# First attention stage: score products by query and by key in 32-row strips, with one PSUM pair for key fills and two for query fills

## The reference, cut to what matters

```python
x = x + 0.5 * ffn(layernorm(x)); x = x + attn(layernorm(x)); ...
Q, K, V = heads(x @ Wq), heads(x @ Wk), heads(x @ Wv)          # 16 heads of 8 features
scores = einsum('bhqd,bhkd->bhqk', Q, K) / sqrt(8)
scores = where(causal_mask, -1e6, scores)
attn = einsum('bhqk,bhkd->bhqd', softmax(scores), V)
return attn.reshape(b, s, 128) @ Wo + bo
```

## Time and profile before

| | |
|---|---|
| runs, us | 2098.77, 2099.65, 2094.84; median 2098.77 |
| the profiled execution's own time | 2099.55 us |
| its span, first to last instruction | 2097.6 us |
| busy over the span | PE 1996.0, PEld 1441.4, DVE 1634.0, ACT 1199.7, POOL 929.9 us |
| the chain that ended last | PE 64%, DVE 11%, issue 10%, POOL 8%, ACT 3% |
| granted TensorE clock, mean | 0.982 of full speed |
| first score product of `attn0` starts | 342.6 us |
| last key product of `attn0` starts | 715.7 us |

### The profile page before, as it was taken

The page is one execution under the profiler, slowest core; times in us unless marked ns, Lnnn a source line. Parts: engine busy times, 40 slices in busy tenths (PEclk is TensorE's granted clock), DMA queues, the critical chain, the costliest instruction groups (busy, mean ns, idle before and its releaser), DMA issues.

```text
span 2097.6 us, 44742 instructions
## 1 busy us (share of the span) xinstructions
PE 1996.0 (95%) x10752; PEld 1441.4 (69%) x10752; DVE 1634.0 (78%) x3337; ACT 1199.7 (57%) x1736; POOL 929.9 (44%) x904
## 2 busy tenths in 40 slices
PE   6999998999999889999999999998999989999998
PEld 4777776666666677777777888875333348877787
DVE  6777777777777667777668888886777788888887
ACT  6667664555555666666544544555766654544444
POOL 4565563333233356666534444442122334444444
PEclk9999999999999999999999999999999999999999
DMA  6233333333333233444301111113343401111112
GB/s 205 95 118 110 103 122 106 98 96 98 90 83 87 64 113 121 120 124 122 113 23 50 46 44 45 45 46 117 99 130 95 125 27 41 46 45 45 40 51 71
DMA packets 120701, 179.29 MB, mean 85 GB/s; under 512 B 33840, under 2 KB 38576, under 8 KB 120496
## 3 DMA queue, kind: packets, MB, share of 16 engines
q1 hardware_dynamic: 120624, 178.37, 27.8%
HBM read 147.10 MB, written 31.20 MB: 85 GB/s over the span
## 4 chain that ended last, share of the span: by engine, by line
PE 64%; DVE 11%; issue 10%; POOL 8%; ACT 3%; DVEq 1%; DMA 1%; SPq 1%; POOLq 1%; ACTq 0%
PE pair L392 14%; PE pair L394 13%; PE pair L393 13%; POOL h_lo L1356 5%; PE bank L644 4%; PE pair L733 3%; PE pair L755 3%; PE bank L622 3%; PE pair L816 2%; PE bank L392 2%; PE bank L394 1%; PE bank L393 1%; DVE rmax L1181 1%; DVE h_hi L1124 1%; POOL h_lo L1362 1%
## 5 line engine op out<-in xcount | busy, mean ns | idle before, releaser
L1362 POOL TENSOR_TENSOR h_lo<-hid,h_hi 128x512 fp32r<-128x512 f32 x256 | 335.5, 1310 | 417.0 <-ACT h_hi L913 416.9
L1356 POOL TENSOR_TENSOR h_lo<-hid,h_hi 128x512 fp32r<-128x512 f32 x256 | 331.6, 1299 | 219.7 <-ACT h_hi L879 219.4
L392 PE MATMUL pair<-xnT_hi,w_hi 128*128 (+1 forms) x1040 | 421.7, 405 | 4.8 <-DVE prod L1103 3.2
L394 PE MATMUL pair<-xnT_hi,w_lo 128*128 (+1 forms) x1040 | 408.7, 393 | 0.0
L393 PE MATMUL pair<-xnT_lo,w_hi 128*128 (+1 forms) x1040 | 408.4, 393 | 0.0
L908 ACT ACTIVATE hid<-pair,bias 128x512 f32<-128x512 f32 x256 | 176.6, 690 | 319.0 <-PE pair L394 276.0
L392 PE MATMUL pair<-h_hi,w_hi 128*128 128x512 f32 x784 | 313.4, 400 | 29.5 <-ACT yT L866 12.6
L394 PE MATMUL pair<-h_hi,w_lo 128*128 128x512 f32 x784 | 307.4, 392 | 0.0
L393 PE MATMUL pair<-h_lo,w_hi 128*128 128x512 f32 x784 | 307.0, 392 | 0.0
L1103 DVE SCALAR_TENSOR_TENSOR prod<-pair,bias,wb 128x512 f32<-128x512 f32 x256 | 191.0, 746 | 76.9 <-PE pair L394 61.4
L1124 DVE TENSOR_SCALAR h_hi<-pair,nb 128x512 fp32r<-128x512 f32 x256 | 191.1, 746 | 75.1 <-PE pair L394 72.3
(11 more groups left out here) (163 smaller groups left out, 3238.8 us busy)
## 6 DMA issues: line engine op xcount, KB each, us to landing
wb<-parts_dram SPq DMA_DIRECT2D x512, 128.0 KB, 2.8
wb<-parts_dram SPq DMA_DIRECT2D x128, 256.0 KB, 3.2
parts_dram<-attn_parts SPq DMA_DIRECT2D x96, 256.0 KB, 3.0
attn_q_st<-parts_dram SPq DMA_DIRECT2D x64, 256.0 KB, 2.7
k_one<-parts_dram SPq DMA_DIRECT2D x128, 64.0 KB, 2.4
attn_k_st<-parts_dram SPq DMA_DIRECT2D x32, 256.0 KB, 3.1
stage_w<-in_w_dram SPq DMA_DIRECT2D x32, 130.0 KB, 2.5
stage_w<-in_w_dram SPq DMA_DIRECT2D x5, 512.0 KB, 6.0
```

What stands on the lines that cost most here:

```text
L392: eng.matmul(o, w_hi_, v_hi, start=start, stop=False, **kw)
L394: return eng.matmul(o, w_lo_, v_hi, start=False, stop=stop, **kw)
L1356: eng.tensor_tensor(h_lo[:, p % NH0, :], hid[:, unit_of(p) % NHID, :] if p else hs[:, :], h_hi[:, p % NH0, :].bitcast(F32), ALU.subtract). ...
L1362: eng.tensor_tensor(h_lo[:, j % NH1, :], hid[:, j // 2 % NHID, :], h_hi[:, j % NH1, :].bitcast(F32), ALU.subtract).then_inc(lo1p_ready, 1)
```

## The change

In `attn0` alone. Each product by query or by key now takes only the 32 rows of its head's strip, for two heads of a fill; the two further heads of fill 4 still take all 128 rows, since they share a bank with the first two. Key fills all use pair 2; query fills and maxima alternate on pairs 0 and 1. In slots of kinds 0 to 3 PE now waits for both pairs and then issues the query fill's two heads and the key fill's two heads, which lie in the four different strips (key fills 2 and 3 have changed places for that, and `pv0` looks its fill up), then the rest of the query fill and the masks. In slots of kind 4 the key fill comes first, and then the query fill. The values of fill 4 come after the key fill, and the maxima move from the middle of kind 4 to the end of kind 3 (`MAX_AT`); on ACT the write-back L918 comes behind the exponential of its slot.

```diff
-K_FILLS = ((0, ((0, 0),)), (1, ((0, 0),)), (0, ((1, P), (3, 0))), (1, ((1, P), (3, 0))), (None, ((2, 0),)))
+K_FILLS = ((0, ((0, 0),)), (1, ((0, 0),)), (1, ((1, P), (3, 0))), (0, ((1, P), (3, 0))), (None, ((2, 0),)))
-MAX_AT = (4, 9, 14, 19)
+MAX_AT = (3, 8, 13, 18)
+QUERY_USES = tuple(u for n in range(NS0) for u in (("q", n),) + ((("max", n),) if n in MAX_AT else ()))
...
-    return (USES.index((what, n % NS0)) - (len(USES) if n < 0 else 0)) % NPAIR
+    return 2 if what == "k" else QUERY_USES.index((what, n % NS0)) % 2
...
+        def wait_pair(eng, ch, use):
+
+            what, n = use
+            if what == "k":
+                if n:
+                    eng.wait_ge(*filled(ch, ("k", n - 1)))
+                elif not ch.first:
+                    eng.wait_ge(*filled(ch.before(), ("k", NS0 - 1)))
+                return
+            for other in reversed(QUERY_USES[:QUERY_USES.index(use)]):
+                if ring(other) == ring(use) and in_chunk(ch, other):
+                    return eng.wait_ge(*filled(ch, other))
...
+        def strip(j):
+            return slice(PC * j, PC * (j + 1))
+
+        def query_scores(eng, quad, fill, j, b, rows_, first=True):
+
+            at0 = 256 * (j // 2) if fill == NF - 1 else 0
+            for i, (qt, at) in enumerate(Q_FILLS[fill][1]):
+                w, at = (qt + 1) * P, at + at0
+                eng.matmul(pair[b][:, j % 2, at:at + w], mem0.q_st[rows_, quad, qt * P:(qt + 1) * P],
+                           mem0.k_one[rows_, quad, j, 0:w], start=(i == 0 and first), stop=True, skip_group_check=True)
...
+            wait_pair(eng, ch, ("k", n))
+            keys, late = list(heads_in(K_FILLS, fill)), n - 1 in MAX_AT
+            if late:
+                for i, j in enumerate(keys):
+                    ins = key_scores(eng, quad, fill, j, ring(("k", n)), strip(j) if i < 2 else slice(0, P), i < 2)
+                ins.then_inc(st_ready, 1)
             if owner is not None:
-                eng.wait_ge(*last_reader(ch, ("q", n)))
-                scores_by_query(eng, owner, f, ring(("q", n)))
-            if n in MAX_AT and in_chunk(ch, ("max", n)):
-                eng.wait_ge(*last_reader(ch, ("max", n)))
-                maxima_to_rows(eng, ch if max_quad(n) < NQ else ch.after(), max_quad(n) % NQ, ring(("max", n)))
+                if f % NF == 0:
+                    eng.wait_ge(st_in[f // NF], stacks_in(owner))
+                wait_pair(eng, ch, ("q", n))
+                queries = list(heads_in(Q_FILLS, f % NF))
+                beside = [j for j in keys if j not in queries[:2]][:2]
+                for j in queries[:2]:
+                    query_scores(eng, f // NF, f % NF, j, ring(("q", n)), strip(j))
+                keys = beside + [j for j in keys if j not in beside]
+            if not late:
+                for i, j in enumerate(keys):
+                    ins = key_scores(eng, quad, fill, j, ring(("k", n)), strip(j) if i < 2 else slice(0, P), i < 2)
+                ins.then_inc(st_ready, 1)
+            if owner is not None:
+                for j in queries[2:]:
+                    query_scores(eng, f // NF, f % NF, j, ring(("q", n)), slice(0, P), False)
+                mask_queries(eng, f % NF, ring(("q", n)))
             if quad and fill == 1:
                 pv0(eng, ch, quad - 1, 2)
-            if n == NF - 1 and ch.first:
-                eng.wait_ge(x_done, ONE + ch.s * NB)
-            eng.wait_ge(*last_reader(ch, ("k", n)))
-            scores_by_key(eng, ch, n, ring(("k", n)))
             if fill == NF - 1:
                 pv0(eng, ch, quad, 0)
                 pv0(eng, ch, quad, 1)
+            if n in MAX_AT and in_chunk(ch, ("max", n)):
+                wait_pair(eng, ch, ("max", n))
+                maxima_to_rows(eng, ch if max_quad(n) < NQ else ch.after(), max_quad(n) % NQ, ring(("max", n)))
```

More of the change, by code:

```diff
@@ L124 @@
 Q_FILLS = ((0, ((3, 0),)), (1, ((3, 0),)), (0, ((2, 0), (0, 384))), (1, ((2, 0), (0, 384))), (None, ((1, 0),)))
-K_FILLS = ((0, ((0, 0),)), (1, ((0, 0),)), (0, ((1, P), (3, 0))), (1, ((1, P), (3, 0))), (None, ((2, 0),)))
+K_FILLS = ((0, ((0, 0),)), (1, ((0, 0),)), (1, ((1, P), (3, 0))), (0, ((1, P), (3, 0))), (None, ((2, 0),)))
 LOAD = 1024
-MAX_AT = (4, 9, 14, 19)
-USES = tuple(u for n in range(NS0) for u in (("q", n),) + ((("max", n),) if n in MAX_AT else ()) + (("k", n),))
-AHEAD_USES = tuple((what, n - NS0) for what, n in USES if n >= NS0 - AHEAD and what != "k" and (what, n) != ("max", MAX_AT[-2]))
+MAX_AT = (3, 8, 13, 18)
+QUERY_USES = tuple(u for n in range(NS0) for u in (("q", n),) + ((("max", n),) if n in MAX_AT else ()))
+AHEAD_USES = tuple((what, n - NS0) for what, n in QUERY_USES if n >= NS0 - AHEAD and (what, n) != ("max", MAX_AT[-2]))
 def max_quad(n):
-    return (n + 1) // NF
+    return (n + 2) // NF
 def ring(use):
     what, n = use
-    return (USES.index((what, n % NS0)) - (len(USES) if n < 0 else 0)) % NPAIR
+    return 2 if what == "k" else QUERY_USES.index((what, n % NS0)) % 2
 class Steps:
@@ L511, in in_chunk @@
             return use[0] == "k" or not ch.last or use[1] < (NS0 - AHEAD if use[0] == "q" else MAX_AT[-1])
[L513 to L518, removed]
+        def wait_pair(eng, ch, use):
[9 more added lines that the diff above has]
+                    return eng.wait_ge(*filled(ch, other))
             if ch.first:
[L520 to L523, removed]
+                what, n = [u for u in AHEAD_USES if ring(u) == ring(use)][-1]
+                return eng.wait_ge(*((s_used, n + AHEAD + 1) if what == "q" else (q_full, 1)))
+            eng.wait_ge(*filled(ch.before(), [u for u in QUERY_USES if ring(u) == ring(use)][-1]))
         def pe_prep(eng, step, ch):
@@ L619, in pv0 @@
                 for j in range(QUAD):
-                    fill = (j // 2, 2 + j // 2, 4)[part]
+                    fill = [heads_in(K_FILLS, f) for f in range(NF)].index(heads_in(K_FILLS, 0 if j < 2 else 1), 2 * part) if part < 2 else 4
                     at = (0, P if kb == 1 else 0, 256 * (j // 2))[part]
@@ L717, in pe_ffn1, with heads_in, key_scores, mask_queries @@
                 down1(eng, ch, j - LAG)
[L719 to L734, removed]
+        def heads_in(fills, fill):
+            which = fills[fill][0]
+            return range(QUAD) if which is None else range(2 * which, 2 * which + 2)
+        def strip(j):
[6 more added lines that the diff above has]
+                           mem0.k_one[rows_, quad, j, 0:w], start=(i == 0 and first), stop=True, skip_group_check=True)
+        def key_scores(eng, quad, fill, j, b, rows_, first=True):
+            at0 = 256 * (j // 2) if fill == NF - 1 else 0
+            for i, (kb, at) in enumerate(K_FILLS[fill][1]):
+                w, at = S - kb * P, at + at0
+                ins = eng.matmul(pair[b][:, j % 2, at:at + w], mem0.k_one[rows_, quad, j, kb * P:(kb + 1) * P],
+                                 mem0.q_st[rows_, quad, kb * P:S], start=(i == 0 and first), stop=True, skip_group_check=True)
+            return ins
+        def mask_queries(eng, fill, b):
             for half in range(2):
@@ L744, in scores_by_query, with query_fill @@
             ins.then_inc(s_ready, 1)
-        def scores_by_key(eng, ch, f, b):
+        def query_fill(eng, ch, f, b):
             quad, fill = f // NF, f % NF
             if fill == 0:
[L750 to L757, removed]
+                eng.wait_ge(st_in[quad], stacks_in(ch))
+            for i, j in enumerate(heads_in(Q_FILLS, fill)):
+                query_scores(eng, quad, fill, j, b, strip(j) if i < 2 else slice(0, P), i < 2)
+            mask_queries(eng, fill, b)
         def maxima_to_rows(eng, ch, quad, b):
@@ L780, in pe_attn0 @@
                     if what == "q":
-                        scores_by_query(eng, ch, m + AHEAD, ring((what, m)))
+                        query_fill(eng, ch, m + AHEAD, ring((what, m)))
                     else:
@@ L786, in pe_attn0 @@
                 f, owner = f - NS0, None if ch.last else ch.after()
-            if owner is not None:
-                eng.wait_ge(*last_reader(ch, ("q", n)))
-                scores_by_query(eng, owner, f, ring(("q", n)))
-            if n in MAX_AT and in_chunk(ch, ("max", n)):
-                eng.wait_ge(*last_reader(ch, ("max", n)))
-                maxima_to_rows(eng, ch if max_quad(n) < NQ else ch.after(), max_quad(n) % NQ, ring(("max", n)))
+            if n == NF - 1 and ch.first:
+                eng.wait_ge(x_done, ONE + ch.s * NB)
+            if fill == 0:
+                eng.wait_ge(q_full, NQ * ch.g + quad + 1)
+            wait_pair(eng, ch, ("k", n))
[4 more added lines that the diff above has]
+                ins.then_inc(st_ready, 1)
+            if owner is not None:
+                if f % NF == 0:
[14 more added lines that the diff above has]
+                mask_queries(eng, f % NF, ring(("q", n)))
             if quad and fill == 1:
                 pv0(eng, ch, quad - 1, 2)
-            if n == NF - 1 and ch.first:
```

(5 more changed lines are left out.)

2 lines of the change are left out of this document (removed).

## The result

The changed kernel takes 2184.16 us (median of 4 runs, 2176.16 to 2191.33), the one before 2098.27 on the same chip (4 runs, 2094.84 to 2099.65). The ratio is 1.0413 with a 95% interval of 1.038 to 1.0447. I had said 2104.5 us, and at most 2127: the sign was right, the size was not.

What follows compares the result with a forecast made beforehand. PE was taken as the bound; 0.65 us more a chunk over seven chunks (4.6) plus 1 for the last took the profiled 2099.55 us to 2105, stated as 2104.5 because the run median is 0.8 lower; range 2088 to 2127.

Steps and rivals of the forecast that it cites:

- the sign: Whole kernel: the forecast time was slower than before, with a chance of 0.50 for slower.
- My own case: Whole kernel: strips save PE time, the new wait spends it; 2104.5 us, within 2097 to 2113; chance 0.47.
- the rival in which it falls: First attention: PE's clock drops to 1.2 GHz at times, adding 8 to 20 us, 2112 to 2125; chance 0.18.
- Four strips in 0.43 us: Score products on PE: four of 512 columns in four strips take 0.43 us, against at least 0.85 in full rows.
- The rival of no overlap: Score products on PE: strips of 32 rows do not overlap at all, adding 50 us, 2150; chance 0.03.
- strict order: PE queue: a second product in a busy strip holds back all behind it, 27 us in all, 2132; chance 0.10.
- The loop: Slots of the stage: strips wait for the previous slot's exponential, so a slot takes at least 1.61 us.
- The quad without other steps: Third quad of a chunk: slots of 1.61, 1.67, 1.61, 1.61 and 3.51 sum to 10.01 us, as before.
- The list of PE's work in the five slots: PE's own work in kinds 0 to 4, given as 8.3 us a quad against 10.0, 54 us if alone.
- Kind 4: Slot with both fills, masks and values: 3.51 us of PE, was 4.04 with the maxima in it.
- the rival "faster": PE: changes between full rows and row strips cost nothing, 1.6 us less a chunk, 2092; chance 0.22.
- DVE and ACT as cover: Stage: DVE with 35 us of 46 stays below the bound; ACT waits 17 us a chunk, so other edits cost nothing.

Runs made afterwards that it cites:

- e1: Kernel before, with only the first two heads of each fill taking 32 rows, by query and by key; 2198.19 us, ratio 1.0474.
- e2: Changed kernel with every product in full rows, keeping its order, pairs and waits; 2158.86 us, ratio 1.0281.
- e3: Changed kernel plus three extra 512-column products over 128 rows ahead of the wait in kinds 1 and 3; 2150.0 us, ratio 1.0221.
- e4: Changed kernel plus three extra 512-column products in the 32 rows of one strip, ahead of the wait in kinds 1 and 3; 2191.4 us, ratio 1.0432.
- e8: Changed kernel with the key fill ahead of the query fill in every slot, both in full rows; 2131.55 us, ratio 1.0164.
- e7: Kernel before, with its three pairs, and the four strips side by side in slots of kind 0 only; 2087.83 us, ratio 0.9948.
- e6: Changed kernel with the key fill ahead of the query fill in every slot, keys in strips, queries in full rows; 2145.86 us, ratio 1.0222.
- e9: Changed kernel plus 4, 2 and 4 extra full-row products ahead of the wait in kinds 1, 2 and 3; 2131.13 us, ratio 1.0154.

## Why the prediction was wrong in size

**The step that failed is the clock.** My own case held it at 1.00 in the stage, so put it at nothing, and the rival in which it falls had 8 to 20 us and a chance of 0.18. The rival had 30 to 55 us of the stage at 1.2 GHz; it was 0.48 x 443 = 213. Its price is the difference between the mean chunk and the one estimated at full clock, 57.2 - 45.3 = 11.9 us. The six chunks in the middle of the stage grew by 6 x (57.2 - 45.75) = 69 of the 86 us, and 6 x 11.9 = 71: there the clock is the whole loss. The first and the last chunk, which have the other 17, I didn't take apart.

Two readings led there. I took the second attention's 0.96 for a like case, without asking how much of its PE time is strips; between its strips of 0.43 us it has longer products of 128 rows. And I gave the standing of PE as the reason for a fall. e1, e2 and the pair e3 and e4 show that strips are a cause of their own: with PE busy 87% of the time at full clock, e1 in strips has 0.72 in the stretch, and e2 in full rows, at 86%, has 1.00. That standing can do its part as well is seen in the last chunk of e2. Whether the second attention's own dips have the same cause no run tested.

**Four strips in 0.43 us: right**, at 0.43 (527.39 to 527.82). The rival of no overlap is out.

**No strict order: right.** In kind 0 the queries' second products of 128 columns start at 534.87, when their strips are free, and the key strips, which the program holds behind them, start at 534.61, 0.02 behind the first query strips. The Trainium skill ("TensorE: Matmul & The Clock Gate", Part 3) has matmuls of different tiles start and end strictly in program order; this trace disagrees, for row strips of unequal length too.

**The loop spends the gain: right, with the terms off both ways.** A slot takes 1.71 us against 1.61: the strips follow the exponential by 0.12, not 0.05, and lead the next by 0.57, not 0.54. The quad without other steps at full clock has 1.71 + 1.89 + 1.72 + 1.94 + 3.07 = 10.3 us where I had 10.01. The other three, which I had followed, come to 11.2, 11.9 and 11.9 where I had 11.87, 12.55 and 12.0. So a chunk would take 45.3 us at full clock where I had 46.4 and the kernel before has 45.75: the single pair all but cancels what the strips save, and nothing in the loop but the clock makes the kernel slower. For the last chunk I had put 1 us. e8, which has the single pair, no strip, and a clock of 0.96 there, takes 45.2 us for it against 39.4 before, so that term is nearer to 5. With it the time at full clock would be near 2100 us, an estimate. That my 2104.5 lies close to it is luck in part, as the two errors have opposite signs. And so is the sign of the forecast: the loop, for which I had the kernel slower, costs next to nothing, and the clock, which I had at nothing, makes the loss.

**Two sums were wrong, without effect on the forecast.** The list of PE's work in the five slots adds up to 7.7 us, not 8.3, so PE alone would have given more than 54 us. And strict order's 0.8 us a quad makes 26 us, so 2130.

**Kind 4: a little better than forecast**, 3.36 us against 3.51. The query strips and the values take 0.43 and 1.85, as forecast; the difference is ahead of the query strips (0.75 against 0.85) and in the masks (0.33 against 0.37). With free changes of mode, as the rival "faster" had it, it would be 3.1. No run tests the changes by themselves.

**DVE and ACT as cover: right.** 34.95 and 25.52 us a chunk, against 35.09 and 25.18; L950 behind its exponential shows nowhere.

My list of what would prove the forecast wrong did name the right rows: a clock of the stage other than 1.00, and a chunk outside 45.5 to 47.5.

## What to carry to other kernels

Products in row strips save PE time where the buffers that they fill are free anyway and most products around them still use all rows: in one slot of five they gave 0.5% (e7), in all five, with nothing else changed, they cost 4.7% (e1). Read the granted clock of the stage, by stretches, before the busy share: a PE that is busy for longer with the same work is often one at half speed. If a fill is to have a single buffer, the reader's instruction and both handovers stand in each slot (1.7 us here), whatever PE saves.

## What the runs showed of the hardware that I had not expected

- TensorE's clock depends on the rows that its products use and not only on whether it is busy. Score products mostly in 32 rows, PE busy 87% at full clock: 0.72 in the stretch (e1); in 128 rows, busy 86%: 1.00 (e2); extra products with 128 rows: 0.76 to 0.85 (e3), the same ones with 32: 0.78 (e4). Score products in strips in all slots, for the keys alone, and in one slot of five: 0.76, 0.95, 1.00 (after, e6, e7). Whether the count of rows matters, the share of the array that works, or that strips run side by side, no run tells apart; e4's filler, one strip by itself, speaks against the last.
- Full rows don't keep the clock up where PE stands more: 0.90 in the last chunk of e2, PE busy 79%.
- Matmuls in free strips start ahead of earlier ones of the program whose strip is busy: 534.61 against 534.87.
- Extra work can be a gain: e3 and e9 have more products than the changed kernel and are 34 and 53 us faster.
- A low stretch costs most where PE has most to do: exponential to exponential over kind 4 took 5.59 us at 1.2 GHz (490.27 to 495.86) and 3.07 at 2.4.
